# Early-fusion block on one core: scores and values of two steps issued together, other PSUM banks, another order of loads

## The chip, the cores and the metric

The kernel runs on one core of a Trainium2 chip. The time is the device time in microseconds (us) of one execution. TensorE (PE) multiplies and transposes into PSUM, which has eight banks of 512 fp32 per partition; VectorE (DVE) and ScalarE (ACT) read PSUM; GpSimd (POOL) works on SBUF; SyncE (SP) only issues transfers. Each engine works through its own list of instructions in order, and semaphores tie the lists together.

## The reference

```python
h = concat([cls, patches(x) @ W.T + b]) + pos_enc      # per image: 1 + 36 tokens
h = concat([h, txt])                                   # T = 114 tokens of D = 256
n = layernorm(h)
q, k, v = n @ Wq, n @ Wk, n @ Wv                       # 16 heads of 64
a = softmax(causal(q @ k.T / 8)) @ v
h = h + (n + a @ Wo)
n = layernorm(h)
gates = softmax(n @ router_w + router_b)               # 8 experts, top 2
# each expert takes up to 570 tokens, in their order
h = h + sum_e gate_e * (gelu(n_e @ w1[e] + b1[e]) @ w2[e] + b2[e])
```

There are 32 images (3 x 96 x 96) with 77 text tokens each. All is fp32; the products of the projections and of the experts are made of three fp32r products each (high x high, low x high, high x low), so each operand is kept as a high and a low part.

## The kernel before

**Groups and steps.** Attention goes over 8 groups of 4 images (`body(g)`, once for every engine). A group has 16 pairs of heads and images and is written as 19 steps `n`. At step `n` PE does four things, in this order: the scores of pair `n` (L1229, into `score_bank`), the values of pair `n - 3` (L1249, into `o_bank`, below also W), the transposes of the probabilities of pair `n - 2` (L1238, into `pT_bank`, below also T), and then a projection (lines L380 to L382, six matmuls of the helper `halves`, into one of three banks `bank`). Up to step 12 that projection is K or Q of a later head pair. The scores are below also S, the projection P.

**Work between the steps.** At step 3 the next group's patches are transposed (jobs E), at step 8 the last group's normalised rows (jobs Y, L1147), at step 12 come the router's logits (job L, L1262), at step 13 the next group's tokens (jobs X, L1147), ahead of that step's scores. Steps 14 to 16 hold the first halves of the next group's V, steps 17 and 18 the second halves (V1, V3 and then V5, V7 as PE counts them). After step 18 come the patch embedding (L1127, into `score_bank0`), the count of places (job C), the output projection (jobs O) and Q, K, Q of the next group.

**The other engines at a step.** ACT at step `n`: the drain of a K projection if `n` is odd, `oT_hi` of pair `n - 3` (L693), the copy `pT` of pair `n - 2` (L697), the four exponentials of pair `n` (L703). At step 9 it also drains a Y job, at step 10 it packs the pixels of group `g + 2` (`tok`, L642). DVE at step `n`: the drain of a Q projection if `n` is even, mask and maximum of pair `n` (L980), `nb` (L984), the reciprocal `rc` of pair `n - 1` (L988), `oT_lo` of pair `n - 3` (L781), then pieces of statistics, normalisation and routing. POOL normalises pair `n - 1` (L570).

**Banks.** `Jobs` lists all jobs that use `bank` in PE's order; job `i` takes bank `i % len(bank)`, and PE waits at its first matmul until job `i - len(bank)` has been drained:

```python
def bank_free(self, name, k):
    i = self.index(name, k) - len(bank)
    return self.emptied(i) if i >= 0 else []
```

**SP.** In the start SP loads the weights and the pixels of groups 0 and 1, then clears the slots in DRAM (8 transfers of 605.6 KB and one of 570 KB, L436 and L437), and then enters `body(0)`: pixels of group 2 (L398, L406), text of group 1 (L409). DVE needs that text at step 7 (statistics of `hraw`).

**Experts.** After the 8 groups the experts' stage runs with all 8 banks; the change only renames its banks.

## Time and profile before

| | |
|---|---|
| median of 3 runs | 967.36 us (965.38 to 967.66) |
| profiled execution | 964.54 us, span 962.6 us, mean granted clock 0.958 |
| PE busy | 869.2 us (90%) |
| DVE, ACT, POOL busy | 555.8, 516.0, 370.4 us |
| chain that ended last | PE 76%, SP's queue 5%, DVE 5%, POOL 4%, ACT 4% |

Busy time is counted by engine; idle time of an engine matters only where another waits for it. The chain that ended last is followed back from the last instruction, at each step to what released it. The step names above are not in the trace: they are found by the order of the rows, since each step has one group of L1229, L1249 and L1238 rows.

### The profile page before, as it was taken

The numbers are of one execution on the slowest core, as the hardware profiler recorded it, in microseconds if no ns is written. First come the engines' busy times: TensorE is split into PE (matmuls) and PEld (weight loads), VectorE is DVE, ScalarE is ACT, GpSimd is POOL, SyncE is SP. The second block draws the span as 40 slices with busy tenths as digits, with TensorE's granted clock in tenths as the row PEclk, the third lists the DMA queues.
The fourth block names the chain that finished last, engine by engine and source line by source line (L and its number), as shares of the span: only waits on it lengthen the run. The fifth ranks groups of instructions, "written<-read, shape, count | busy, mean of one in ns | idle before, by whom it ended". The sixth has DMA issues, their size and how long they took to land.

```text
span 962.6 us, 19817 instructions
## 1 busy us (share of the span) xinstructions
PE 869.2 (90%) x6897; PEld 753.9 (78%) x6897; DVE 555.8 (58%) x2433; ACT 516.0 (54%) x1686; POOL 370.4 (38%) x677
## 2 busy tenths in 40 slices
PE   4895899999999999999999999998617999999996
PEld 3674697788778779778877877876617999999996
DVE  3563428645753853764575375476326777777771
ACT  3373808825952880782495288087005555555551
POOL 2132305426425534542642554454430333222333
PEclk9797999999999999999999999999757999999998
DMA  8442101102011111110200110100125654444422
GB/s 253 118 131 78 39 1 35 38 13 64 11 29 44 33 38 39 37 39 8 59 1 1 33 35 2 37 1 2 24 90 165 165 124 127 96 131 109 94 26 25
DMA packets 61907, 57.64 MB, mean 60 GB/s; under 512 B 26783, under 2 KB 56651, under 8 KB 61696
## 3 DMA queue, kind: packets, MB, share of 16 engines
q1 hardware_dynamic: 41170, 45.15, 15.3%
q0 software_dynamic: 18944, 9.76, 6.3%
q10 hardware_dynamic: 1696, 1.49, 0.6%
q8 instruction: 55, 0.90, 0.4%
q14 instruction: 42, 0.34, 0.1%
HBM read 34.25 MB, written 21.89 MB: 58 GB/s over the span
## 4 chain that ended last, share of the span: by engine, by line
PE 76%; SPq 5%; DVE 5%; POOL 4%; ACT 4%; issue 3%; DMA 2%; ACTq 1%; POOLq 0%; DVEq 0%
PE bank L380 13%; PE bank L382 12%; PE bank L381 12%; PE pT_bank L1238 6%; PE o_bank L1249 6%; PE score_bank L1229 6%; PE score_bank L1127 3%; SPq L436 3%; POOL pr L570 2%; PE o_bank L380 2%; PE o_bank L381 2%; PE o_bank L382 2%; PE score_bank L380 2%; PE score_bank L381 2%; PE score_bank L382 2%
## 5 line engine op out<-in xcount | busy, mean ns | idle before, releaser
L570 POOL TENSOR_SCALAR pr<-pr,rc 114x114 f32<-114x114 f32 x512 | 179.3, 370 | 244.9 <-DVE rc L988 244.9
L703 ACT ACTIVATE pr<-sm,nb 114x114 f32<-114x114 f32 x512 | 192.2, 379 | 34.9 <-DVE nb L984 33.5
L980 DVE CUSTOM_DVE_ANT_0 sm<-score_bank,mask 114x114 f32<-114x114 f32 x512 | 110.5, 272 | 52.9 <-PE score_bank L1229 52.8
L601 POOL DMA_INDIRECT out_dram<-yout,dest x40 | 74.0, 1851 | 164.0 <-ACT yout L755 162.5
L551 POOL DMA_INDIRECT slots_dram<-rows,slot x64 | 72.8, 1138 | 128.0 <-DVE slot L947 93.3
L621 ACT ACTIVATE kT<-bank 128x456 f32<-128x456 f32 x64 | 34.1, 533 | 146.8 <-PE bank L382 146.8
L1229 PEld LDWEIGHTS score_bank<-kT,qT 64*114 64x114 f32 x1024 | 61.8, 176 | 56.7 <-issue 34.7
L380 PE MATMUL bank<-xT_hi,wqkv_hi 128*128 128x456 f32 x256 | 104.0, 406 | 0.0
L1229 PE MATMUL score_bank<-kT,qT 64*114 64x114 f32 x1024 | 84.5, 283 | 20.6 <-DVE mx L980 17.5
L703 ACT ACTIVATION_READ_ACCUMULATOR pr<-sm,nb 114x1 f32 x512 | 97.1, 190 | 0.0
L381 PE MATMUL bank<-xT_lo,wqkv_hi 128*128 128x456 f32 x256 | 94.5, 369 | 0.0
L382 PE MATMUL bank<-xT_hi,wqkv_lo 128*128 128x456 f32 x256 | 94.5, 369 | 0.0
L1238 PE MATMUL pT_bank<-ident,pr 114*114 114x114 f32 x512 | 78.3, 276 | 10.3 <-POOL pr L570 10.3
L697 ACT ACTIVATE pT<-pT_bank 114x456 f32<-114x456 f32 x128 | 70.6, 551 | 23.2 <-PE pT_bank L1238 23.0
L1249 PE MATMUL o_bank<-pT,vv 114*64 114x114 f32 x1024 | 79.5, 277 | 2.3 <-ACT pT L697 2.1
L1238 PEld LDWEIGHTS pT_bank<-ident,pr 114*114 114x114 f32 x512 | 49.6, 136 | 30.5 <-POOL pr L570 14.5
L380 PE MATMUL bank<-wo_hi,oT_hi 128*114 128x256 f32 x256 | 73.1, 286 | 0.0
L382 PE MATMUL bank<-wo_hi,oT_lo 128*114 128x256 f32 x256 | 72.6, 283 | 0.0
L381 PE MATMUL bank<-wo_lo,oT_hi 128*114 128x256 f32 x256 | 72.4, 283 | 0.0
L693 ACT ACTIVATE oT_hi<-o_bank 128x228 fp32r<-128x228 f32 x128 | 45.7, 357 | 47.0 <-PE o_bank L1249 47.0
L1249 PEld LDWEIGHTS o_bank<-pT,vv 114*64 114x64 f32 x1024 | 51.1, 138 | 23.0 <-issue 8.1
L781 DVE TENSOR_TENSOR oT_lo<-o_bank,oT_hi 128x228 fp32r<-128x228 f32 x128 | 47.9, 374 | 33.9 <-ACT oT_hi L693 33.4
(198 smaller groups left out, 2227.0 us busy)
## 6 DMA issues: line engine op xcount, KB each, us to landing
stage_a<-in_L_ffn_w_dram SPq DMA_DIRECT2D x8, 1024.0 KB, 5.1
stage_b<-in_L_ffn_w_dram SPq DMA_DIRECT2D x8, 1024.0 KB, 7.2
slots_dram<-fill SPq DMA_DIRECT2D x8, 605.6 KB
xs<-slots_dram SPq DMA_DIRECT2D x8, 605.6 KB
pix<-in_x_dram SPq DMA_DIRECT2D x96, 36.0 KB, 2.2
hraw<-in_txt_dram SPq DMA_DIRECT2D x8, 308.0 KB
out_dram<-h SPq DMA_DIRECT2D x8, 308.0 KB
pix<-pix SPq DMA_DIRECT2D x7, 216.0 KB, 2.5
```

The source lines that it names most:

```text
L380: pe.matmul(out_ap, a[0], b[0], start=start, stop=False)
L381: pe.matmul(out_ap, a[0], b[1], start=False, stop=False)
L382: return pe.matmul(out_ap, a[1], b[0], start=False, stop=stop)
L551: pool.indirect_dma_start(slots, bass.IndirectOffsetOnAxis(ap=slot[:, j, b:b + 1], axis=0), rows[k % 2][:, b, :], None, bounds_check=E * C ...
L570: p = pool.tensor_scalar(pr[:, m % 4, i, :], pr[:, m % 4, i, :], rc[:, m % 4, i:i + 1], 1.0, ALU.mult, ALU.mult)
L601: pool.indirect_dma_start(out, bass.IndirectOffsetOnAxis(ap=dest[e % 2][:, t:t + 1], axis=0), yout[:, t, :], None, compute_op=ALU.add).the ...
L697: act.activation(pT[:, m % 2, :, :], pT_bank[0:T, 0:4 * T].rearrange("p (i q) -> p i q", i=4), ACT.Copy).then_inc(pT_copied, 1)
L703: a = act.activation(pr[:, n % 4, i, :], sm[:, n % 2, i, :], ACT.Exp, bias=nb[:, n % 2, i:i + 1], scale=SCALE, accum_out=rs[:, n % 4, i:i ...
L980: m = dve.tensor_tensor_reduce(sm[:, n % 2, i, :], score_bank[i % 2][0:T, i // 2 * T:(i // 2 + 1) * T], mask[:, :], 1.0, NEG, ALU.add, ALU ...
L1229: m = pe.matmul(score_bank[h][0:T, b * T:(b + 1) * T], qT[head, c % 2, tokens], kT[head, c % 2, tokens], start=True, stop=True)
L1238: m = pe.transpose(pT_bank[0:T, i * T:(i + 1) * T], pr[:, n % 4, i, :], ident[0:T, 0:T])
L1249: m = pe.matmul(o_bank[n % 2][h * DK:(h + 1) * DK, b * T:(b + 1) * T], vv[:, b0 + b, v0:v0 + DK], pT[:, n % 2, 2 * b + h, :], start=True, ...
```

## The change

`bank` has two banks instead of three, and `pT_bank` two instead of one. PE issues scores at even steps only, for pairs `n` and `n + 1`, into 456 columns of each score bank instead of 228, and values at even steps only, for pairs `n - 4` and `n - 3`; ACT and DVE take `oT_hi` and `oT_lo` of the same two pairs at even steps. DVE's maximum of a pair waits for the scores of both. DVE drains all four second halves of V at step 18 instead of two at step 17 and two at step 18. SP loads each group's text ahead of the pixels, and clears the slots inside `body(0)`, behind both.

```diff
@@ -198,9 +198,9 @@
         def psum(name):
             return ctx.enter_context(nc.psum_tensor(name, [128, 512], F32))
-        bank = [psum(f"bank{i}") for i in range(3)]
+        bank = [psum(f"bank{i}") for i in range(2)]
         score_bank = [psum(f"score_bank{i}") for i in range(2)]
-        pT_bank = psum("pT_bank")
+        pT_bank = [psum(f"pT_bank{i}") for i in range(2)]
         o_bank = [psum(f"o_bank{i}") for i in range(2)]
@@ -247,7 +247,7 @@
         AT_E, AT_Y, AT_L, AT_X = 3, 8, 12, 13
         V_FIRST = {AT_X + 1: (0,), AT_X + 2: (1, 2), AT_X + 3: (3,)}
-        V_SECOND = {PAIRS + 1: (0, 1), PAIRS + 2: (2, 3)}
+        V_SECOND, V_DRAINED = {PAIRS + 1: (0, 1), PAIRS + 2: (2, 3)}, {PAIRS + 2: (0, 1, 2, 3)}
         STATS2, MOMENTS2, NORM2 = {1: (0, 1), 2: (2, 3)}, 3, {5: (0, 1), 6: (2, 3)}
         STATS1, MOMENTS1, NORM1 = {7: (0, 1), 8: (2, 3)}, 8, {10: (0, 1), 11: (2, 3)}
@@ -345,7 +345,7 @@
-        ebanks = bank + score_bank + [pT_bank] + o_bank
+        ebanks = bank + score_bank + pT_bank + o_bank
@@ -431,19 +431,22 @@
             sp.dma_start(router_bb[:, :, :], router_b.rearrange("(o b e) -> o b e", o=1, b=1).broadcast_to([T, GB, E])).then_inc(small_in, 16)
             sp.wait_ge(packed, 1)
             load_pixels(1)
-            sp.wait_ge(fill_done, 2)
-            for e in range(E):
-                sp.dma_start(slots[e * CAP:(e + 1) * CAP, :].rearrange("(t p) r -> p t r", p=T), fill[:, :, :]).then_inc(slots_cleared, 16)
-            sp.dma_start(out[B * T:B * T + CAP, :].rearrange("(t p) r -> p t r", p=T), fill[:, :, 0:D]).then_inc(slots_cleared, 16)
+            def clear_slots():
+                sp.wait_ge(fill_done, 2)
+                for e in range(E):
+                    sp.dma_start(slots[e * CAP:(e + 1) * CAP, :].rearrange("(t p) r -> p t r", p=T), fill[:, :, :]).then_inc(slots_cleared, 16)
+                sp.dma_start(out[B * T:B * T + CAP, :].rearrange("(t p) r -> p t r", p=T), fill[:, :, 0:D]).then_inc(slots_cleared, 16)
             def body(g, first=False, last=False):
                 jobs = Jobs(g)
+                if not last:
+                    sp.wait_ge(hx_done, 2 * g + 2)
+                    load_text(g + 1)
                 if g < G - 2:
                     sp.wait_ge(packed, g + 2)
                     load_pixels(g + 2)
-                if not last:
-                    sp.wait_ge(hx_done, 2 * g + 2)
-                    load_text(g + 1)
+                if first:
+                    clear_slots()
                 if not first:
                     wait_all(sp, jobs.emptied(jobs.last_before("O", 1)))
                     set_out(g - 1)
@@ -679,22 +682,22 @@
                                 drain_x(jobs, k)
                         for b in V_FIRST.get(n - 1, ()):
                             drain_v(jobs, b)
-                    if 3 <= n:
-                        m = n - 3
-                        c, b = m // 2, 2 * (m % 2)
-                        if first and m == 0:
-                            act.wait_ge(filled, len(START_JOBS))
-                            act.wait_ge(wk_lo, 1)
-                            act.wait_ge(wo_lo_done, 1)
-                            act.wait_ge(cls_in, 16)
-                        act.wait_ge(o_done, pair(g, m + 1))
-                        act.activation(oT_hi[:, c, b * T:(b + 2) * T], o_bank[m % 2][:, 0:2 * T], ACT.Copy).then_inc(o_hi, 1)
+                    if first and n == 4:
+                        act.wait_ge(filled, len(START_JOBS))
+                        act.wait_ge(wk_lo, 1)
+                        act.wait_ge(wo_lo_done, 1)
+                        act.wait_ge(cls_in, 16)
+                    if n % 2 == 0:
+                        for m in (n - 4, n - 3):
+                            if 0 <= m:
+                                c, b = m // 2, 2 * (m % 2)
+                                act.wait_ge(o_done, pair(g, m + 1))
+                                act.activation(oT_hi[:, c, b * T:(b + 2) * T], o_bank[m % 2][:, 0:2 * T], ACT.Copy).then_inc(o_hi, 1)
                     if 2 <= n < PAIRS + 2:
                         m = n - 2
                         act.wait_ge(pT_done, pair(g, m + 1))
-                        act.activation(pT[:, m % 2, :, :], pT_bank[0:T, 0:4 * T].rearrange("p (i q) -> p i q", i=4), ACT.Copy).then_inc(pT_copied, 1)
+                        act.activation(pT[:, m % 2, :, :], pT_bank[m % 2][0:T, 0:4 * T].rearrange("p (i q) -> p i q", i=4), ACT.Copy).then_inc(pT_copied, 1)
                     if n < PAIRS:
                         act.wait_ge(bias_done, pair(g, n + 1))
                         if not (first and n < 4):
@@ -975,9 +978,9 @@
                             drain_x(jobs, k)
                     if n < PAIRS:
-                        dve.wait_ge(scores_done, 2 * pair(g, n + 1))
+                        dve.wait_ge(scores_done, 2 * pair(g, n + 2 - n % 2))
                         for i in range(4):
-                            m = dve.tensor_tensor_reduce(sm[:, n % 2, i, :], score_bank[i % 2][0:T, i // 2 * T:(i // 2 + 1) * T], mask[:, :],
+                            m = dve.tensor_tensor_reduce(sm[:, n % 2, i, :], score_bank[i % 2][0:T, (2 * (n % 2) + i // 2) * T:(2 * (n % 2) + i // 2 + 1) * T], mask[:, :],
                                                          1.0, NEG, ALU.add, ALU.max, mx[:, n % 2, i:i + 1])
                         m.then_inc(max_done, 1)
                         dve.wait_ge(max_done, pair(g, n + 1))
@@ -986,12 +989,12 @@
                         dve.wait_ge(exp_done, pair(g, n))
                         dve.reciprocal(rc[:, (n - 1) % 4, :], rs[:, (n - 1) % 4, :]).then_inc(recip_done, 1)
-                    if 3 <= n:
-                        m = n - 3
-                        c, b = m // 2, 2 * (m % 2)
-                        dve.wait_ge(o_hi, pair(g, m + 1))
-                        split_low(oT_lo[:, c, b * T:(b + 2) * T], o_bank[m % 2][:, 0:2 * T], oT_hi[:, c, b * T:(b + 2) * T], o_lo)
+                    if n % 2 == 0:
+                        for m in (n - 4, n - 3):
+                            if 0 <= m:
+                                c, b = m // 2, 2 * (m % 2)
+                                dve.wait_ge(o_hi, pair(g, m + 1))
+                                split_low(oT_lo[:, c, b * T:(b + 2) * T], o_bank[m % 2][:, 0:2 * T], oT_hi[:, c, b * T:(b + 2) * T], o_lo)
                     if not first:
                         for b in STATS2.get(n, ()):
                             statistics(b, h2, st2, stats2)
@@ -1016,7 +1019,7 @@
                             dve.wait_ge(hx_done, 2 * g + 2)
                         for b in NORM1.get(n, ()):
                             normalise(b, xn[:, b, :], hraw[:, b, :], mv1, rstd1, xn_done)
-                        for b in V_SECOND.get(n, ()):
+                        for b in V_DRAINED.get(n, ()):
                             drain_v(jobs, b)
                 if not last and not (isinstance(g, int) and g == G - 2):
                     drain_embedded(g + 2)
@@ -1217,25 +1220,25 @@
                     wait_all(pe, jobs.emptied(jobs.last_before("K", 0) if c == 0 else jobs.index("K", c)))
                     wait_all(pe, jobs.emptied(jobs.last_before("Q", c) if c < 2 else jobs.index("Q", c)))
-                if n == 0 and g < G - 1:
-                    pe.wait_ge(embT_done, g + 2)
-                else:
-                    pe.wait_ge(max_done, pair(g, n))
+                    if n == 0 and g < G - 1:
+                        pe.wait_ge(embT_done, g + 2)
+                    else:
+                        pe.wait_ge(max_done, pair(g, n))
                 for b in range(2):
                     tokens = slice((b0 + b) * T, (b0 + b + 1) * T)
                     for h in range(2):
                         head = slice(h * DK, (h + 1) * DK)
-                        m = pe.matmul(score_bank[h][0:T, b * T:(b + 1) * T], qT[head, c % 2, tokens], kT[head, c % 2, tokens], start=True, stop=True)
+                        m = pe.matmul(score_bank[h][0:T, tokens], qT[head, c % 2, tokens], kT[head, c % 2, tokens], start=True, stop=True)
                         if b == 1:
                             m.then_inc(scores_done, 1)
             def transpose_probs(g, n, first):
                 pe.wait_ge(normed, pair(g, n + 1))
-                if not (first and n < 1):
-                    pe.wait_ge(pT_copied, pair(g, n))
+                if not (first and n < 2):
+                    pe.wait_ge(pT_copied, pair(g, n - 1))
                 for i in range(4):
-                    m = pe.transpose(pT_bank[0:T, i * T:(i + 1) * T], pr[:, n % 4, i, :], ident[0:T, 0:T])
+                    m = pe.transpose(pT_bank[n % 2][0:T, i * T:(i + 1) * T], pr[:, n % 4, i, :], ident[0:T, 0:T])
                 m.then_inc(pT_done, 1)
             def weigh_values(g, n, first):
@@ -1279,10 +1282,14 @@
                         pe.wait_ge(xn_done, GB * (g + 2))
                         for k in range(KC):
                             transpose_tokens(jobs, "X", xn, k)
-                    if n < PAIRS:
-                        scores(g, n, jobs, first)
-                    if 3 <= n:
-                        weigh_values(g, n - 3, first)
+                    if n % 2 == 0:
+                        for m in (n, n + 1):
+                            if m < PAIRS:
+                                scores(g, m, jobs, first)
+                        for m in (n - 4, n - 3):
+                            if 0 <= m:
+                                weigh_values(g, m, first)
                     if 2 <= n < PAIRS + 2:
                         transpose_probs(g, n - 2, first)
                     if n < LAST_QK:
```

What stands in a row of PE's list at step 18 of a steady group, before (pair 15's values, then V5 and the first matmul of V7; "waits" names the semaphores, `act_drained` and `dve_drained` count drained jobs):

```order
L1249 MATMUL o_bank1<-pT_80,vv_77 64x114 [waits o_lo,pT_copied]
L1249 MATMUL o_bank1<-pT_80,vv_77 64x114 x3
L380 MATMUL bank1<-wqkv_hi_60,xT_hi_73 114x512 [waits act_drained]
L381 MATMUL bank1<-wqkv_lo_61,xT_hi_73 114x512
L382 MATMUL bank1<-wqkv_hi_60,xT_lo_74 114x512
L380 MATMUL bank1<-wqkv_hi_60,xT_hi_73 114x512
L381 MATMUL bank1<-wqkv_lo_61,xT_hi_73 114x512
L382 MATMUL bank1<-wqkv_hi_60,xT_lo_74 114x512
L380 MATMUL bank2<-wqkv_hi_60,xT_hi_73 114x512 [waits dve_drained]
```

and now, with the values of pairs 14 and 15 ahead of V5 and V7:

```order
L1252 MATMUL o_bank0<-pT_80,vv_77 64x114 [waits o_lo,pT_copied]
L1252 MATMUL o_bank0<-pT_80,vv_77 64x114 x3
L1252 MATMUL o_bank1<-pT_80,vv_77 64x114 [waits o_lo,pT_copied]
L1252 MATMUL o_bank1<-pT_80,vv_77 64x114 x3
L380 MATMUL bank0<-wqkv_hi_60,xT_hi_73 114x512 [waits dve_drained]
L381 MATMUL bank0<-wqkv_lo_61,xT_hi_73 114x512
L382 MATMUL bank0<-wqkv_hi_60,xT_lo_74 114x512
L380 MATMUL bank0<-wqkv_hi_60,xT_hi_73 114x512
L381 MATMUL bank0<-wqkv_lo_61,xT_hi_73 114x512
L382 MATMUL bank0<-wqkv_hi_60,xT_lo_74 114x512
L380 MATMUL bank1<-wqkv_hi_60,xT_hi_73 114x512 [waits dve_drained]
```

V5 waited for a drain of ACT (V6, three jobs back); it now waits for a drain of DVE (V1, two jobs back).

DVE's list at the same place, before, from the drains of V1 and V3 at step 17 on (`vv` is V, the rows with `chosen` and `before` are the routing of step 18):

```order
L785 COPY vv_77<-bank2 114x512 [waits filled,routed]
L785 COPY vv_77<-bank0 114x512 [waits filled]
L781 TENSOR_TENSOR oT_lo_82<-o_bank1,oT_hi_81 128x228 [waits o_hi]
L928 TENSOR_TENSOR chosen_110<-oh_109 114x32
L931 TENSOR_TENSOR before_111<-before_111,chosen_110 114x8 [waits routed] x4
L785 COPY vv_77<-bank1 114x512 [waits filled]
L785 COPY vv_77<-bank2 114x512 [waits filled]
```

and now:

```order
L784 TENSOR_TENSOR oT_lo_82<-o_bank0,oT_hi_81 128x228 [waits o_hi,routed]
L784 TENSOR_TENSOR oT_lo_82<-o_bank1,oT_hi_81 128x228 [waits o_hi]
L931 TENSOR_TENSOR chosen_110<-oh_109 114x32
L934 TENSOR_TENSOR before_111<-before_111,chosen_110 114x8 [waits routed] x4
L788 COPY vv_77<-bank0 114x512 [waits filled]
L788 COPY vv_77<-bank1 114x512 [waits filled]
L788 COPY vv_77<-bank0 114x512 [waits filled]
L788 COPY vv_77<-bank1 114x512 [waits filled]
```

The drains of V1 and V3 have moved behind both `oT_lo` and behind the routing of step 18.

PE's list at steps 13 and 14 of a steady group, before, from the second X transposes to the scores of pair 14:

```order
L1147 MATMUL bank0<-ident_49,xn_70 128x114 [waits act_drained]
L1147 MATMUL bank0<-ident_49,xn_70 128x114 x3
L1229 MATMUL score_bank0<-kT_76,qT_75 114x114 [waits max_done]
L1229 MATMUL score_bank1<-kT_76,qT_75 114x114
L1229 MATMUL score_bank0<-kT_76,qT_75 114x114
L1229 MATMUL score_bank1<-kT_76,qT_75 114x114
L1249 MATMUL o_bank0<-pT_80,vv_77 64x114 [waits o_lo,pT_copied]
L1249 MATMUL o_bank0<-pT_80,vv_77 64x114 x3
L1238 MATMUL pT_bank<-ident_49,pr_79 114x114 [waits pT_copied,normed]
L1238 MATMUL pT_bank<-ident_49,pr_79 114x114 x3
L1229 MATMUL score_bank0<-kT_76,qT_75 114x114 [waits max_done,dve_drained,act_drained]
L1229 MATMUL score_bank1<-kT_76,qT_75 114x114
```

and now (the scores of pair 13 stand a step earlier, those of 14 and 15 together):

```order
L1150 MATMUL bank0<-ident_49,xn_70 128x114 [waits act_drained,xn_done]
L1150 MATMUL bank0<-ident_49,xn_70 128x114 x3
L1150 MATMUL bank1<-ident_49,xn_70 128x114 [waits dve_drained]
L1150 MATMUL bank1<-ident_49,xn_70 128x114 x3
L1241 MATMUL pT_bank1<-ident_49,pr_79 114x114 [waits pT_copied,normed]
L1241 MATMUL pT_bank1<-ident_49,pr_79 114x114 x3
L1232 MATMUL score_bank0<-kT_76,qT_75 114x114 [waits max_done,dve_drained,act_drained]
L1232 MATMUL score_bank1<-kT_76,qT_75 114x114
L1232 MATMUL score_bank0<-kT_76,qT_75 114x114
L1232 MATMUL score_bank1<-kT_76,qT_75 114x114
```

Between the X transposes and the scores of pair 14, which wait for DVE's maximum of pair 13, only one group of transposes is left where three groups of work stood.

## Rows read from the trace of the kernel before

**Rows 1.** The page's first line.

```profile
span 962.6 us, 19817 instructions
```

**Rows 2.** Timeline of SP's queue, 25 to 90 us: start, length, line, issues.

```profile
33.34 29.74 SPq L436 DMA_DIRECT2D slots_dram<-fill  x8
...
68.18 12.10 SPq L398 DMA_DIRECT2D pix<-in_x_dram  x12
...
82.34 0.53 SPq L409 DMA_DIRECT2D hraw<-in_txt_dram  x1
```

**Rows 3.** Timeline of DVE in group 0; in brackets the idle time before.

```profile
85.83 0.75 DVE L806 BATCH_NORM_STATS2 st<-hraw 114x6 f32<-114x256 f32 x2 [13.06 <-DMA hraw<-in_txt_dram]
```

**Rows 4.** Timeline of PE in group 0: scores of steps 8, 9 and 14.

```profile
87.95 1.11 PE L1229 MATMUL score_bank<-kT,qT 64*114 64x114 f32 x8 [11.45 <-DVE mx L980]
...
92.83 0.66 PE L1229 MATMUL score_bank<-kT,qT 64*114 64x114 f32 x8
...
106.86 0.66 PE L1229 MATMUL score_bank<-kT,qT 64*114 64x114 f32 x8 [2.10 <-DVE mx L980]
```

**Rows 5.** Timeline of PE, one steady group from its first scores to the next group's.

```profile
304.83 0.66 PE L1229 MATMUL score_bank<-kT,qT 64*114 64x114 f32 x8
...
324.58 0.66 PE L1229 MATMUL score_bank<-kT,qT 64*114 64x114 f32 x8
...
325.17 0.61 PE L1249 MATMUL o_bank<-pT,vv 114*64 114x114 f32 x8
...
325.71 0.60 PE L1238 MATMUL pT_bank<-ident,pr 114*114 114x114 f32 x4
...
327.49 0.66 PE L1229 MATMUL score_bank<-kT,qT 64*114 64x114 f32 x8
...
334.11 0.66 PE L1229 MATMUL score_bank<-kT,qT 64*114 64x114 f32 x8
...
340.51 0.66 PE L1229 MATMUL score_bank<-kT,qT 64*114 64x114 f32 x8 [0.52 <-ACT kT L621]
...
344.95 1.08 PE L1147 MATMUL bank<-ident,xn 114*128 114x114 f32 x8
...
348.33 0.66 PE L1229 MATMUL score_bank<-kT,qT 64*114 64x114 f32 x8 [0.63 <-DVE mx L980]
...
350.38 0.47 PE L380 MATMUL bank<-wqkv_hi,xT_hi 128*114 128x512 f32 x1
...
363.24 0.50 PE L380 MATMUL bank<-wqkv_hi,xT_hi 128*114 128x512 f32 x1
...
366.12 4.08 PE L1127 MATMUL score_bank<-tok,embW 96*128 96x144 f32 x32
...
385.38 0.66 PE L1229 MATMUL score_bank<-kT,qT 64*114 64x114 f32 x8
```

**Rows 6.** Instructions of line L1229, 320 to 330 us: min/median/max ns.

```profile
L1229 PE MATMUL score_bank<-kT,qT x24: 258/260/350, 321.7 to 327.9; 64*114 64x114 f32 x24
```

**Rows 7.** Timeline of ACT in the same group.

```profile
326.35 0.55 ACT L697 ACTIVATE pT<-pT_bank 114x456 f32<-114x456 f32 x1 [0.16 <-PE pT_bank L1238]
...
335.88 0.55 ACT L697 ACTIVATE pT<-pT_bank 114x456 f32<-114x456 f32 x1 [0.16 <-PE pT_bank L1238]
...
337.82 2.20 ACT L642 ACTIVATE tok<-pix 96x1152 f32<-96x1152 f32 x1
...
339.93 0.53 ACT L621 ACTIVATE kT<-bank 128x456 f32<-128x456 f32 x1
```

**Rows 8.** Timeline of POOL in the same group.

```profile
326.56 1.39 POOL L570 TENSOR_SCALAR pr<-pr,rc 114x114 f32<-114x114 f32 x4 [1.44 <-DVE rc L988]
```

**Rows 9.** Timeline of DVE in the same group, at step 18.

```profile
363.75 0.40 DVE L781 TENSOR_TENSOR oT_lo<-o_bank,oT_hi 128x228 fp32r<-128x228 f32 x1 [0.25 <-ACT oT_hi L693]
364.06 0.18 DVE L928 TENSOR_TENSOR chosen<-oh 114x32 bf16<-114x32 f32 x1
364.28 0.75 DVE L931 TENSOR_TENSOR before<-before,chosen 114x8 bf16<-114x8 bf16 x4
364.95 0.68 DVE L785 COPY vv<-bank 114x512 f32<-114x512 f32 x1
```

## The prediction

> **What bounds the kernel now.** I read the page first, then SP's queue, then PE's timeline in group 0 and in one steady group, then ACT, POOL and DVE beside it. The span is 962.6 us [rows 1]. In group 0 DVE sat idle 13.06 us until the text of group 1 had landed [rows 3]; its issue stands at 82.34 us, behind the slot clearing (29.74 us for eight issues from 33.34 on, then one more) and 12.10 us of pixel issues [rows 2]. PE waited 11.45 us for DVE's maximum, and its scores then took 1.11 us a block instead of 0.66: step 8 lasted from 87.95 to 92.83, 4.88 us [rows 4]. In a steady group PE is the bound: 80.55 us from 304.83 to 385.38, and a plain step (324.58 to 327.49) is 2.91 us: scores 0.59, values 0.54, transposes with a projection 1.78, with no wait [rows 5]. Only two kinds of waits show in its rows: 0.52 us for ACT's drain of K (after the packing) and 0.63 us for DVE's maximum (after the X jobs) [rows 5]. So what the change saves on PE counts, but what it makes PE wait for counts as well.
>
> **Text ahead of clearing.** The nine clearing transfers and the pixels no longer stand ahead of the text. The text goes out when `hx` of group 0 is made; SP has nothing else queued ahead of it, and DVE first looks for it at 72.8 us (85.83 less 13.06) [rows 3]. The wait of 11.45 us goes, and the half clock behind it: step 8 costs 2.91 instead of 4.88 us [rows 4, 5]. Gain 11.45 + 1.97 = 13.4 us. The clearing now lies beside groups 0 and 1; behind it on SP stand the text of group 2 and group 0's output, wanted a group later. Cost nothing; without that cover it would cost what the text costs now.
>
> **What merging saves on PE.** A block of scores has 8 matmul records; the row is 0.66 us long, one record lasts 0.26 [rows 5, 6], so their starts lie 0.40 / 7 = 0.057 us apart and 8 of them fill 0.46 us, while a block takes 0.59. Values in the same way: (0.61 - 0.26) / 7 x 8 = 0.40 of 0.54. A second block behind one of its kind should cost 0.46 and 0.40. Two steps then take 0.59 + 0.46 + 0.54 + 0.40 + 2 x 1.78 = 5.55 us instead of 5.82. Bounds: the gap may belong to every block (saves 0), or the gap between projection and scores may go too (some 0.1 more). I take 0.27.
> The Trainium skill (TensorEngine Tiling (Array Packing), Key Properties) says that changing the tiling mode drains TensorE. Scores use 64-row tiles, values 64-column ones, transposes the whole array; by that rule a merged pair has three changes fewer and takes about 5.45 us, and if the gap belonged to every block instead it would take 5.82. No row separates the two.
>
> **What takes it back in a plain pair of steps.** POOL's normalisation of pair n - 1 starts 1.98 us after the scores of step n (326.56 against 324.58) and lasts 1.39 [rows 5, 8], since DVE takes the reciprocal behind the maximum of pair n. That maximum now waits for both blocks, 0.46 later: 1.98 + 0.46 + 1.39 + 0.06 = 3.89 us, where PE wants those transposes at 1.05 + 0.94 + 1.78 = 3.77. A pair of steps takes 3.89 + 1.78 = 5.67, only 0.15 less than before.
> ACT loses slack. At an even step its two `oT_hi` and `pT` wait for values and transposes of PE, which start at 1.05 + 0.94 = 1.99. `pT` starts 0.64 later (325.71 to 326.35), the exponentials end 1.94 after its start (335.88 to 337.82) [rows 5, 7]: 4.57, and the drain of K behind them 0.53 + 0.05: 5.15, against 4.3 before. That is in time for 5.67, but not for the four places below. Times count from a block of scores; S0, S10 are the scores of pairs 0, 10.
>
> - **S0 to S10, before 29.28 us.** The first exponentials start 0.46 later and the transposes of pairs 0 and 1 with them; nothing lies ahead to hide it. At step 3 the second E job needs Q's bank, issued just before it. Together about +0.55, each partly hidden. At step 8 the second Y job takes the bank of the K just issued, drained only at 5.15 where PE wants it at 4.2; with 0.44 for the transposes and 1.78 that makes a pair of 7.37. Two plain pairs and this: 18.7 against 18.25, +0.5.
> - **S10 to S12, before 6.40.** ACT packs pixels for 2.11 us (337.82 to 339.93) ahead of K's drain [rows 7]: 5.15 + 2.11 = 7.26. +0.86, in groups 0 to 5.
> - **S12 to the first V, before 9.87.** One more block of scores and of values go ahead of X: 4.44 + 0.86 = 5.30. From X to the scores of pair 14 it stays 3.38 us (344.95 to 348.33), which ends with DVE's maximum of pair 13 behind both `xT_lo`; but PE has only one group of transposes left to do in it, and waits some 2.0 (3.38 less 1.0 of X and 0.37) instead of 0.63 [rows 5]. Then 1.99 + 0.37. Sum 11.04, +1.17.
> - **First V to the embedding, before 15.74 (350.38 to 366.12).** Gone from it: scores of pair 15 (0.59) and twice 0.14: 14.87. New: V5 needs V1's bank, which DVE drains behind both `oT_lo` and the routing. Before, V5 started at 363.24 and `oT_lo` of pair 15 at 363.75, 0.51 later; the routing ends 1.20 after that (364.95), the drain takes 0.68 [rows 5, 9]. PE waits 0.51 + 1.20 + 0.68 + 0.06 = 2.45. Sum 17.32, +1.58. V7, C, O and the next Q and K find their banks drained: 1.4 us or more of PE's work lies between each and its drain. The 19.26 us to the next group stay.
>
> Groups 1 to 5: 0.55 + 0.5 + 0.86 + 1.17 + 1.58 = 4.66 each, 23.3. Group 0 has no Y job, no logits and no routing: 0.55 - 0.4 + 0.86 + 0.7 + 0.7 = 2.4. Group 6 doesn't pack: 3.7. Group 7 has neither X nor V: about 1.1 (Y, and pairs 14 and 15 later behind the logits). Sum 30.5 us; the second `pT` bank saves nothing, since `pT` was copied in time. Stages outside attention are left as they are.
>
> **Sum.** 964.54 + 30.5 - 13.4 = 981.6 us, against the profiled execution's own time, which lies 2.8 us under the median of the runs; I forecast 983.
>
> **Rivals.**
> (a) As worked out: 983, its own range 972 to 994 (merging saves nothing: 64 pairs x 0.27 = 17, of which waits already swallow about half, +9; waits in part hidden: -11). Chance 0.52.
> (b) The same, and the waits also cost the clock. After 11.45 us of idling the granted clock was at its lower level and a step cost 1.97 more; after 2.10 us of idling scores still took 0.66 [rows 4]. The waits of 2.45 us (groups 1 to 6) lie between these. If each of the six is followed by such a stretch: +12, 995; if the seven of 2.0 as well: 1008. Chance 0.15. The Trainium skill (TensorE: Matmul & The Clock Gate, HAM oscillation) names idle gaps between bursts of matmuls as what puts the array back to half clock; by it these waits could do so.
> (c) Faster: merged blocks on PE are cheaper than their records' pace. Everything above hangs on the start of the even step's transposes, so a saving of x more in each pair of blocks comes back 64 times (8 a group). From x = 0.25 the change is even, from 0.30 measurably faster; with x = 0.4, 983 - 26 = 957. Against it: the second blocks would have to cost 0.46 together, and records 0.057 apart show no room. For it: the change of shape between blocks may cost more than rows show. Chance 0.18, with all other ways to less than 13 us of loss in it.
> (d) Losses and the gain cancel: if the wait for V1 and the one after X cost half, 30.5 becomes 17, 968. Chance 0.10.
> (e) The text move does nothing, since something else holds step 7 of group 0 (the `hx` release, or SP's issues): 983 + 13 = 996. Against it: rows 2 and 3 name transfer and place. Chance 0.05.
>
> **Numbers.** A measurement of this kernel tells about 0.3%, 2.9 us. Faster 0.18 (c), same 0.10 (d), slower 0.72 (a, b, e). The range leaves out the far half of (b) and the far third of (c): 956 to 1000.
>
> **What the changed kernel's profile would show.** Text: DVE's wait of 13 us at step 7 of group 0 is gone, the text issues ahead of the pixels and of the clearing. Merging: rows of scores x16 about 1.1 us long, values starting 1.05 after them; a plain pair of steps near 5.67 us with a small wait of PE for POOL at the odd step. Waits of PE: for ACT's K drain at step 8 (about 1.0) and at step 12 (1.6), for DVE's maximum at step 14 (2.0), for DVE's drain of V1 at step 18 (2.45, and 1.6 in group 0). A steady group of 85.2 us. Wrong if: the steady group is under 82.5 us, the granted clock leaves its full level in groups 1 to 6, or the wait at step 18 is under 1 us.

## The result, and the profile after

The changed kernel takes **1002.4 us** (median of 4 runs, 999.36 to 1003.81) against 967.25 for the kernel before on the same chip: ratio 1.0363, 95% interval 1.0336 to 1.0390. It is 35 us slower, where the forecast of 983 us meant 16, and lies above its range of 956 to 1000. The profiled execution is 997.4 us long, 34.8 more than before [rows 1].

The page of the changed kernel: span, busy times, granted clock in 40 slices, the chain that ended last, and two groups of PE rows with their idle time.

```profile
span 997.4 us, 19801 instructions
...
PE 867.5 (87%) x6897; PEld 764.9 (77%) x6897; DVE 553.2 (55%) x2433; ACT 515.2 (52%) x1686; POOL 371.8 (37%) x677
...
PEclk9899999999899989989998999999755999999999
...
PE 74%; DVE 8%; ACT 6%; issue 5%; POOL 4%; DMA 1%; SPq 1%; POOLq 0%; DVEq 0%; ACTq 0%
...
L1232 PE MATMUL score_bank<-kT,qT 64*114 64x114 f32 x1024 | 71.5, 281 | 26.9 <-DVE mx L983 14.9
...
L380 PE MATMUL bank<-wqkv_hi,xT_hi 128*114 128x512 f32 x128 | 59.6, 465 | 17.2 <-DVE vv L788 15.7
```

PE waits 14.9 us for DVE's maximum ahead of scores and 15.7 us for DVE's drains of V. SP's queue, 5% of the chain before, is down to 1%. The PEclk line is the first sign of something that the sum did not hold: one slice with an 8 in each of groups 2 to 5, where the kernel before has none.

SP's queue, 50 to 110 us, to be read against [rows 2]:

```profile
58.05 0.32 SPq L409 DMA_DIRECT2D hraw<-in_txt_dram  x1
58.41 7.69 SPq L398 DMA_DIRECT2D pix<-in_x_dram  x12
...
68.25 30.20 SPq L437 DMA_DIRECT2D slots_dram<-fill  x8
98.48 4.87 SPq L438 DMA_DIRECT2D out_dram<-fill  x1
```

The text goes out at 58.05 instead of 82.34, and DVE's wait of 13.06 us is gone; that part of the change does what it says. Now the time by groups, each from its first scores to the next group's. A row gives start and end, length, then busy time and count of PE, its weight loads, DVE, ACT and POOL, then the granted clock, the DMA share and GB/s. Before (groups 0, 1 and 6, then group 7 with all that follows; groups 2 to 5 read like 1):

```profile
50.80:143.75 92.95, 77.66 (x611) 63.29 (x610) 38.87 (x209) 46.41 (x175) 25.85 (x67) 0.93 0.21 61
143.75:224.29 80.54, 78.16 (x635) 64.27 (x634) 47.32 (x252) 47.34 (x177) 36.16 (x76) 1.00 0.13 34
...
546.47:622.43 75.96, 74.00 (x604) 60.26 (x603) 47.01 (x251) 45.47 (x176) 36.12 (x76) 1.00 0.08 21
622.43:962.60 340.17, 293.02 (x2355) 280.92 (x2354) 211.56 (x681) 170.21 (x436) 117.82 (x123) 0.91 0.34 84
```

The changed kernel (groups 2, 4 and 5 read like 3):

```profile
51.05:133.79 82.74, 74.64 (x611) 62.43 (x610) 38.67 (x209) 46.58 (x175) 25.93 (x67) 0.98 0.28 83
133.79:218.31 84.52, 75.50 (x636) 63.73 (x635) 46.81 (x252) 46.93 (x177) 36.43 (x76) 1.00 0.12 32
...
307.07:395.80 88.73, 79.69 (x635) 67.16 (x635) 47.11 (x252) 47.33 (x177) 36.30 (x76) 0.94 0.12 31
...
573.29:656.39 83.10, 74.40 (x603) 62.19 (x602) 46.54 (x251) 45.05 (x176) 36.31 (x76) 0.96 0.08 20
656.39:997.40 341.01, 289.96 (x2355) 279.97 (x2354) 210.88 (x681) 170.17 (x436) 117.82 (x123) 0.92 0.34 84
```

Group 0 is 10.2 us shorter, group 1 is 4.0 longer at full clock, groups 2 to 5 are 8.2 longer each with a granted clock of 0.94, group 6 is 7.1 longer; start and tail give 1.1. Sum: -10.2 + 4.0 + 32.8 + 7.1 + 1.1 = 34.8.

**Group 1 against group 3.** Group 1 shows the waits alone. Its four stretches that the forecast names (S0 to S10, S10 to S12, to the first V, to the embedding), in the same columns:

```profile
133.79:163.92 30.13, 27.02 (x238) 21.70 (x237) 22.99 (x135) 22.56 (x92) 13.58 (x34) 1.00 0.22 57
163.92:171.11 7.19, 5.63 (x53) 4.46 (x52) 5.57 (x30) 6.91 (x22) 5.40 (x13) 1.00 0.00 0
171.11:181.95 10.84, 8.86 (x107) 8.00 (x107) 5.63 (x38) 8.47 (x34) 2.77 (x8) 1.00 0.01 2
181.95:199.04 17.09, 14.72 (x95) 10.94 (x94) 8.63 (x41) 8.43 (x30) 4.16 (x12) 1.00 0.00 1
```

PE in it:

```profile
161.71 0.51 PE L1150 MATMUL bank<-ident,rows 114*128 114x114 f32 x3 [0.91 <-ACT kT L624]
...
171.11 1.06 PE L1232 MATMUL score_bank<-kT,qT 64*114 64x114 f32 x16 [1.18 <-ACT kT L624]
...
179.66 1.06 PE L1232 MATMUL score_bank<-kT,qT 64*114 64x114 f32 x16 [1.98 <-DVE mx L983]
...
196.17 0.49 PE L380 MATMUL bank<-wqkv_hi,xT_hi 128*114 128x512 f32 x1 [2.37 <-DVE vv L788]
196.50 0.40 PE L381 MATMUL bank<-wqkv_lo,xT_hi 128*114 128x512 f32 x1
...
199.04 0.65 PE L1130 MATMUL score_bank<-tok,embW 96*128 96x144 f32 x4
```

These are the four waits that the forecast names: second Y job, step 12, pair 14, V5. Beside them stand one of 0.58 us for ACT at step 2 and one of 0.98 for POOL at step 3, inside the first stretch. The same places in group 3, where the waits are as long but the work behind them is not:

```profile
352.94 1.89 PE L1232 MATMUL score_bank<-kT,qT 64*114 64x114 f32 x16 [1.97 <-DVE mx L983]
354.76 1.79 PE L1252 MATMUL o_bank<-pT,vv 114*64 114x114 f32 x16
...
372.10 0.49 PE L380 MATMUL bank<-wqkv_hi,xT_hi 128*114 128x512 f32 x1 [2.37 <-DVE vv L788]
...
373.58 0.63 PE L381 MATMUL bank<-wqkv_lo,xT_hi 128*114 128x512 f32 x1
...
376.55 0.66 PE L1130 MATMUL score_bank<-tok,embW 96*128 96x144 f32 x4
```

The same 16 score matmuls last 1.89 us instead of 1.06, a V matmul 0.63 instead of 0.40. The clock granted there:

```profile
352.00:359.00 7.00, 6.06 (x41) 5.18 (x42) 3.90 (x32) 3.80 (x17) 2.77 (x8) 0.51 0.00 0
359.00:370.00 11.00, 10.73 (x77) 7.99 (x75) 4.02 (x21) 7.08 (x24) 2.77 (x8) 1.00 0.01 1
372.00:376.00 4.00, 3.90 (x10) 2.90 (x11) 1.33 (x3) 0.00 (x0) 0.00 (x0) 0.57 0.00 0
```

Half clock (1.2 GHz) for 6.8 us at the scores of pair 14 and for 3.4 us at V5, full clock (2.4 GHz) between. In slices of 1 us the first fall comes at 352.1, after 1.1 us of the wait and 0.8 ahead of the scores; the second comes at 372.6, 0.5 behind V5's start. From the scores of pair 14 to V5 group 1 needs 196.17 - 179.66 = 16.51 us, group 3 19.16: the first stretch costs 2.65. From V5 to the embedding 2.87 against 4.45: the second costs 1.58. Together 4.23, which is all of the difference of the two groups, 88.73 - 84.52. Both falls show in groups 2 to 5; group 0 has one of 3.4 us, group 6 two of 3.4, group 1 none.

### The profile page after: what moved, and what is told of

Read it like the earlier page. It is cut to its first block, busy times and chain, and to the rows that moved or that the text cites. A ratio compares the mean times of both kernels' runs of the same rounds, so it can differ in the third digit from the quotient of the medians.

```text
span 997.4 us, 19801 instructions
## 1 busy us (share of the span) xinstructions
PE 867.5 (87%) x6897; PEld 764.9 (77%) x6897; DVE 553.2 (55%) x2433; ACT 515.2 (52%) x1686; POOL 371.8 (37%) x677
## 3 DMA queue, kind: packets, MB, share of 16 engines
q1 hardware_dynamic: 41170, 45.15, 14.9%
## 4 chain that ended last, share of the span: by engine, by line
PE 74%; DVE 8%; ACT 6%; issue 5%; POOL 4%; DMA 1%; SPq 1%; POOLq 0%; DVEq 0%; ACTq 0%
PE bank L380 11%; PE bank L382 11%; PE bank L381 11%; PE score_bank L1232 7%; PE o_bank L1252 5%; PE pT_bank L1241 5%; ACT pr L706 4%; PE score_bank L1130 3%; POOL pr L573 3%; DVE sm L983 3%; PE pT_bank L380 2%; PE pT_bank L381 2%; PE pT_bank L382 2%; PE o_bank L381 2%; PE o_bank L382 2%
## 5 line engine op out<-in xcount | busy, mean ns | idle before, releaser
L1232 PE MATMUL score_bank<-kT,qT 64*114 64x114 f32 x1024 | 71.5, 281 | 26.9 <-DVE mx L983 14.9
L1241 PE MATMUL pT_bank<-ident,pr 114*114 114x114 f32 x512 | 79.1, 279 | 16.2 <-POOL pr L573 14.9
L1241 PEld LDWEIGHTS pT_bank<-ident,pr 114*114 114x114 f32 x512 | 53.0, 139 | 42.3 <-POOL pr L573 31.4
L380 PE MATMUL bank<-wqkv_hi,xT_hi 128*114 128x512 f32 x128 | 59.6, 465 | 17.2 <-DVE vv L788 15.7
L1252 PE MATMUL o_bank<-pT,vv 114*64 114x114 f32 x1024 | 69.5, 282 | 0.3 <-ACT pT L700 0.3
L784 DVE TENSOR_TENSOR oT_lo<-o_bank,oT_hi 128x228 fp32r<-128x228 f32 x128 | 44.5, 381 | 35.5 <-ACT oT_hi L696 35.5
```

The costliest lines, as they stand in the source:

```text
L380: pe.matmul(out_ap, a[0], b[0], start=start, stop=False)
L1232: m = pe.matmul(score_bank[h][0:T, tokens], qT[head, c % 2, tokens], kT[head, c % 2, tokens], start=True, stop=True)
L1241: m = pe.transpose(pT_bank[n % 2][0:T, i * T:(i + 1) * T], pr[:, n % 4, i, :], ident[0:T, 0:T])
L1252: m = pe.matmul(o_bank[n % 2][h * DK:(h + 1) * DK, b * T:(b + 1) * T], vv[:, b0 + b, v0:v0 + DK], pT[:, n % 2, 2 * b + h, :], start=True, ...
```

## The experiments

**The theories.** Clock theory: the four waits cost their length, as the forecast had it, and two of them, being idle, also bring PE's clock down. First rival: the half clock has another cause (the merged blocks, the load over time), and filling the waits changes nothing. Second rival: waits cost only their length, and the rest lies elsewhere. All times are medians of 4 runs or more, taken on several chips; the kernel before took 966.6 to 968.1 beside them, and the ratios are to that.

**SP's order alone.** The kernel before with the text and the clearing moved as in the change's diff, nothing else.

```diff
             load_pixels(1)
-            sp.wait_ge(fill_done, 2)
...
             def body(g, first=False, last=False):
                 jobs = Jobs(g)
+                if not last:
+                    sp.wait_ge(hx_done, 2 * g + 2)
+                    load_text(g + 1)
                 if g < G - 2:
                     sp.wait_ge(packed, g + 2)
                     load_pixels(g + 2)
...
+                if first:
+                    clear_slots()
```

> The kernel before with nothing but SP's new order: text ahead of pixels and of the clearing. By the forecast DVE's wait of 13.06 us for the text, PE's of 11.45 us behind it and the half clock after it (1.97 us) go: 967.3 - 13.4 = 954 us. Rival: something else holds step 7 of group 0, and the time stays at 967. The changed kernel's group 0 was only 10.2 us shorter than before, but that holds merged steps as well.

Measured 954.8 us, ratio 0.9866 [0.9847, 0.9885], against 967.7: -12.9 where -13.4 was forecast. The group of 92.95 us became 81.63, 11.3 less, since a half clock that was not there before now follows the wait ahead of pair 14 in it:

```profile
96.10 1.12 PE L1232 MATMUL score_bank<-kT,qT 64*114 64x114 f32 x8 [2.11 <-DVE mx L983]
```

(In the profiled executions the start, up to the first scores, is 2.8 us longer and the whole 9.0 shorter; it is the medians that differ by 12.9.) So all else in the change costs 1002.4 - 954.8 = 47.6 us, not the 30.5 of the sum.

**Waits filled with work.** The changed kernel, with matmuls in the two longest waits.

```diff
+            def fillers(dst, count):
+                for _ in range(count):
+                    pe.matmul(dst[:, :], wqkv_hi[:, 0, 0:128], wqkv_hi[:, 0, 0:512], start=True, stop=True)
...
+                if n == 14 and g < G - 1 and 7:
+
+                    pe.wait_ge(o_lo, pair(g, 10))
+                    fillers(o_bank[0], 7)
...
+                            if b == 2:
+                                pe.wait_ge(max_done, pair(g, PAIRS))
+                                fillers(score_bank[1], 8)
                             project_v(jobs, 2 * b + 1)
```

> The changed kernel with idle time on PE filled: 7 matmuls of 512 columns whose result nobody reads stand ahead of the scores of pair 14, and 8 ahead of V5. They wait for nothing new and take about 0.22 us each, so they lie inside the waits of 1.97 and 2.37 us. Clock theory: those waits, being idle, bring the granted clock to half for 6.7 and 3.4 us behind them in groups 2 to 5, which costs 88.75 - 84.52 = 4.23 us a group, some 3.5 in group 6 and 1.5 in group 0; with matmuls in them the clock stays full and the time is 1002.4 - 22 = 980 us. Rival: the half clock comes from something else (the merged blocks, the whole load over time); then it stays and so does the time, 1002 us or a little more.

Measured 980.2 us, ratio to before 1.0128 [1.0107, 1.0149]: 22.2 us less than the changed kernel although PE does 105 matmuls more. PE in its group 3, then its groups 1 and 3:

```profile
346.10 1.85 PE L1219 MATMUL o_bank<-wqkv_hi 128*128 128x512 f32 x7
348.31 1.06 PE L1240 MATMUL score_bank<-kT,qT 64*114 64x114 f32 x16 [0.36 <-DVE mx L983]
...
362.38 2.14 PE L1219 MATMUL score_bank<-wqkv_hi 128*128 128x512 f32 x8
364.83 0.49 PE L380 MATMUL bank<-wqkv_hi,xT_hi 128*114 128x512 f32 x1 [0.31 <-DVE vv L788]
```

```profile
133.30:217.86 84.56, 79.16 (x650) 66.36 (x649) 46.87 (x252) 46.96 (x177) 36.56 (x76) 1.00 0.12 32
302.42:386.94 84.52, 79.16 (x650) 66.34 (x649) 46.86 (x252) 46.95 (x177) 36.45 (x76) 1.00 0.12 33
```

Groups 1 to 5 now take 84.5 us each, and the granted clock is 1.00 in groups 0 to 6. The scores of pair 14 and V5 start as long after the group's first scores as they did in group 1 of the changed kernel (45.9 and 62.4 us); only the idling is gone. That rules out the first rival: the merged blocks are all there. The second goes as well. The kernel without the half clock is the one that the forecast costed, and it takes 980 where 983 was said. (The profiled executions differ by 18.9 us and not 22.2: that of the changed kernel is the fastest of its four.)

**Only V5's wait filled.** The same without the 7 matmuls.

> The changed kernel with the 8 filling matmuls ahead of V5 alone; the wait of 1.97 us ahead of the scores of pair 14 stays idle. Clock theory, one fall for each wait: the half clock of 3.4 us behind V5 goes (1.6 us each in groups 2 to 6), that of 6.8 us behind pair 14 stays: 1002.4 - 8 = 994. If the two waits bring the clock down only together, both falls go: 980.

Measured 994.6 us, ratio 1.0283 [1.0265, 1.0301]. The clock around V5 is full in every group (in group 3, 370 to 376 us: 1.00); at the scores of pair 14 it still falls, for 3.4 or 6.8 us, now in group 1 as well. So a fall needs only one of the two waits: filling V5's took 7.8 us off, filling that of pair 14 as well another 14.4.

**V1 and V3 drained first at step 18.** DVE drains them behind the values of pair 15, ahead of both `oT_lo` and the routing.

```diff
-        V_SECOND, V_DRAINED = {PAIRS + 1: (0, 1), PAIRS + 2: (2, 3)}, {PAIRS + 2: (0, 1, 2, 3)}
+        V_SECOND, V_DRAINED = {PAIRS + 1: (0, 1), PAIRS + 2: (2, 3)}, {PAIRS + 2: (2, 3)}
...
+                    if not last and n == PAIRS + 2:
+                        dve.wait_ge(o_done, pair(g, PAIRS))
+                        drain_v(jobs, 0)
+                        drain_v(jobs, 1)
                     if n % 2 == 0:
                         for m in (n - 4, n - 3):
```

> The changed kernel, but at step 18 DVE drains V1 and V3 right behind the values of pairs 14 and 15, ahead of both oT_lo and of the routing. The wait ahead of V5 falls from 2.37 to some 0.9 us, 1.4 less in groups 1 to 6 and 0.7 less in group 0: -9 us, 993, if waits cost only their length. If the half clock behind this wait (1.6 us each in groups 2 to 6) goes with it: -17 us, 985.

Measured 984.8 us (977.69 to 986.34), ratio 1.0155 [1.0112, 1.0199]. V5 in a steady group, then the clock at the scores of pair 14 and at V5:

```profile
367.22 0.48 PE L380 MATMUL bank<-wqkv_hi,xT_hi 128*114 128x512 f32 x1 [0.85 <-DVE vv L788]
```

```profile
348.00:355.00 7.00, 5.16 (x38) 4.53 (x39) 4.57 (x32) 3.42 (x14) 2.79 (x8) 0.53 0.00 0
366.00:371.00 5.00, 4.15 (x28) 3.27 (x25) 3.93 (x11) 0.72 (x2) 0.00 (x0) 1.00 0.00 0
```

V5's wait is 0.85 us, and no half clock follows in any group; pair 14 still has it in groups 0 to 6. V1 cannot be drained at step 17, as it was before: its half of V is what the values of pair 14 still read, and merging has put these into step 18. So the wait for V1 comes from merging as well as from the banks.

**Maximum of pair 13 first.** At step 13 DVE does maximum, `nb` and reciprocal ahead of the logits and of both `xT_lo`.

```diff
-                    if not first and n == AT_L + 1:
-                        route(jobs, g - 1, 0)
-                    if not last and n == AT_X:
-                        for k in range(KC):
-                            drain_x(jobs, k)
                     if n < PAIRS:
...
                     if 1 <= n <= PAIRS:
...
                         dve.reciprocal(rc[:, (n - 1) % 4, :], rs[:, (n - 1) % 4, :]).then_inc(recip_done, 1)
+                    if not first and n == AT_L + 1:
+                        route(jobs, g - 1, 0)
+                    if not last and n == AT_X:
+                        for k in range(KC):
+                            drain_x(jobs, k)
```

> The changed kernel, but at step 13 DVE takes the maximum of pair 13 and the reciprocal of pair 12 ahead of the logits and of both xT_lo. The wait ahead of the scores of pair 14 falls from 1.97 to some 0.3 us; X's drains come about 1 us later, which V0 doesn't see. -1.6 us in seven groups: 991, if waits cost only their length. If the half clock behind this wait (2.65 us each in groups 2 to 6, some 1.5 in group 0) goes too: -26 us, 977.

Measured 969.5 us, ratio 1.0024 [1.0010, 1.0038], 7 less than expected. The scores of pair 14 wait for nothing, and V5, in a steady group, as long as ever. The clock at V5 follows, in that group (3) and in group 4:

```profile
343.84 1.06 PE L1232 MATMUL score_bank<-kT,qT 64*114 64x114 f32 x16
...
360.50 0.50 PE L380 MATMUL bank<-wqkv_hi,xT_hi 128*114 128x512 f32 x1 [2.38 <-DVE vv L788]
```

```profile
360.00:364.00 4.00, 3.50 (x18) 2.85 (x19) 2.16 (x4) 0.00 (x0) 0.00 (x0) 1.00 0.00 0
444.00:448.00 4.00, 4.00 (x14) 3.00 (x13) 0.94 (x2) 0.00 (x0) 0.00 (x0) 0.57 0.02 4
```

Here the clock mostly holds behind the same wait of 2.38 us: it fell in groups 1 and 4 only, against groups 2 to 6 in the changed kernel, and groups 2, 3 and 5 took 82.63 to 82.65 us. The three falls fewer are worth 3 x 1.58 = 4.7 of the 7 us. The length of a wait alone does not decide.

**Both orders of DVE.**

> The changed kernel with both reorderings of DVE together (maximum of pair 13 ahead of the logits and of xT_lo; V1 and V3 drained ahead of oT_lo and routing). In the run with the first alone a group took 82.65 us where the clock held, with the wait of 2.38 ahead of V5; in the run with the second alone that wait was 0.85. So 82.65 - 1.53 = 81.1 us a group, and no half clock: 969.5 - 7 x 1.5 - 3 = 956 us. If the clock falls for another reason than these two waits, 960 to 965.

Measured 957.4 us, ratio 0.9888 [0.9870, 0.9906], 81.3 to 81.9 us a steady group, granted clock 1.00 in groups 0 to 6. As expected, and already 1.1% faster than before, with banks and merging as in the change.

**The banks alone.** SP's new order, and the banks two and two, steps not merged.

```diff
-        bank = [psum(f"bank{i}") for i in range(3)]
+        bank = [psum(f"bank{i}") for i in range(2)]
-        pT_bank = psum("pT_bank")
+        pT_bank = [psum(f"pT_bank{i}") for i in range(2)]
```

> The kernel before with SP's new order (954.8 us) and the banks of the changed kernel (two and two), steps not merged, V drained as before. If the banks alone bring the waits ahead of the second E and the second Y (0.29 and 0.91 us in the changed kernel): 954.8 + 7 x 1.2 = 963. If those waits come from ACT's later drains under merging, nothing: 955. The wait ahead of V5 can't come back here, since V1 is drained a step earlier.

Measured 976.4 us, ratio 1.0086 [1.0069, 1.0102]: 21.5 above SP's order alone, where 8 were expected at most. Waits of PE in its group 2, and the clock behind the last of them (one of 0.74 us for POOL, which the kernel before has too, and one of 0.55 near the group's end are not shown):

```profile
227.62 0.61 PE L1142 MATMUL bank<-ident,embT 128*36 128x128 f32 x4 [0.29 <-DVE qT L788]
...
244.08 0.61 PE L1150 MATMUL bank<-ident,rows 114*128 114x114 f32 x4 [0.92 <-ACT kT L624]
...
253.94 0.66 PE L1232 MATMUL score_bank<-kT,qT 64*114 64x114 f32 x8 [0.52 <-ACT kT L624]
...
258.94 0.97 PE L1150 MATMUL bank<-ident,xn 114*128 114x114 f32 x8 [0.41 <-ACT kT L624]
```

```profile
260.00:267.00 7.00, 7.00 (x45) 5.37 (x46) 4.00 (x24) 4.94 (x21) 2.77 (x8) 0.54 0.01 2
```

The waits for E and Y are those of the changed kernel, and with three banks they are gone (below), so they belong to the banks. I had not expected one ahead of X, nor that group 1 would take 83.01 us at full clock (2.47 more, of which the waits make 1.7), nor half clock behind the X jobs of groups 2 and 3 (group 0 has it with SP's order alone as well). Groups 2 to 5 took 336.8 us together, 4 x 2.47 + 4.7 above before: 4.4 of the last term is the half clock of two of them. Another 3.3 us lie behind group 6 (343.0 us against 339.7 with SP's order alone), where the granted clock from 670 to 702 us was 0.68 against 0.84 at the same place (651 to 683).

**Merging alone.** The changed kernel with three projection banks and one for transposed probabilities.

> The changed kernel with the banks of before (three for projections, one for transposed probabilities) and nothing else: merged steps, text ahead, DVE's order as it is. Against the run with both reorderings of DVE (939.4) the wait of 1.97 us ahead of the scores of pair 14 comes back in seven groups (+12) and, by the clock theory, the half clock of 6.8 us behind it (2.65 us in six groups, +16); V5 has no wait, since its bank is V6's, drained by ACT. 967 us. If the clock holds with this one wait, 952. The fourth corner of a square with the kernel with SP's order alone (954.8), that with the two-and-two banks (976.4) and the changed kernel (1002.4).

Measured 973.1 us, ratio 1.0066 [1.0043, 1.0090]; 967 was expected. The clock falls at the scores of pair 14 in groups 1 to 6, and the last V job waits 0.80 us for DVE, which I had left out. In its group 0 the wait ahead of pair 14 is 2.71 us, more than in any other of these kernels, and the granted clock stayed at 1.00. The four kernels with SP's new order can now be set side by side: neither banks nor merging 954.8, banks alone +21.5, merging alone +18.3, both +47.6, that is 7.8 more than the two added.

**Merging with three banks and both orders of DVE.**

> The same, and the banks of before: three for projections, one for transposed probabilities; steps merged by two as in the changed kernel. Tells what the banks cost from what the merging costs. The waits that hang on a projection bank go (0.29 ahead of the second E, 0.91 ahead of the second Y, 0.85 ahead of V5): 81.1 - 2.05 = 79.05 us a group against 80.55 before, 956 - 14 = 942 us. Rival: with one pT bank the transposes of the odd step wait for ACT's copy of the even one (0.5 us in each of 8 pairs of steps): 956 - 14 + 28 = 970.

Measured **939.4 us**, ratio 0.9709 [0.9693, 0.9725], 78.93 us a steady group. The rival of 970 us is ruled out: with one `pT_bank` PE waits nowhere for ACT's copy in a steady group, so a second one saves nothing, as the forecast had it. One wait stands out, at step 12:

```profile
323.06 1.06 PE L1236 MATMUL score_bank<-kT,qT 64*114 64x114 f32 x16 [1.44 <-ACT kT L624]
```

**The packing at step 16 as well.** Besides three banks, merging and both orders of DVE:

```diff
-        AT_PACK = 10
+        AT_PACK = 16
```

> The fastest so far (three banks, merged, both reorderings of DVE, 939.4 us) with ACT's packing of pixels (2.11 us) at the end of step 16 instead of step 10. The wait for K's drain ahead of the scores of pair 12, 1.44 us in six groups, goes, since the drain then comes where the forecast put it without packing, 5.15 us after the even step's scores: -8 us, 931. If the packing then delays V6's drain or pT of pair 15 behind it, as much comes back in steps 17 and 18: 939.

Measured **929.5 us**, ratio 0.9611 [0.9595, 0.9627], the fastest kernel of the study, 3.9% faster than the kernel before. The wait at step 12 is gone and nothing took its place; a steady group:

```profile
282.15:359.62 77.47, 75.18 (x636) 63.77 (x635) 47.01 (x252) 46.64 (x177) 36.40 (x76) 1.00 0.13 36
```

**What merging is worth when nothing takes it back.** First SP's order with the maximum of pair 13 first, not merged, three banks.

> The kernel before with SP's new order and with the maximum of pair 13 ahead of the logits and of xT_lo on DVE; no merging, banks as before. The wait ahead of the scores of pair 14, 0.63 us in groups 1 to 6, shrinks to nothing: -3.8. In group 0 of the run with SP's order alone it was 2.11 us, and 6.82 us at half clock followed: -1.6 - 2.5. Sum 947 us. If POOL's normalisation of pair 12 takes the place of that wait, 952 to 955.

Measured 946.1 us, ratio 0.9777 [0.9761, 0.9794]. Then with the packing at step 16, which leaves merging (with the drain of V that it forces) as the only difference to the 929.5 us.

> The kernel before with SP's new order, the maximum of pair 13 first on DVE, and the packing at step 16; steps not merged, three banks and one. It is the 929.5 us kernel without the merging. The 0.52 us wait for K's drain at step 12 goes: 946.05 - 3.1 = 943. By the forecast merging saves 0.27 us in a pair of steps where nothing takes it back, 8 pairs of steps in 8 groups: 17 us; by the measured plain pairs (5.66 against 5.82) 10 us. So the merged kernel should be 10 to 17 us faster than this one. If its gain came from the banks or orders alone, this one takes 930 as well.

Measured 941.8 us, ratio 0.9729 [0.9713, 0.9745]; a steady group:

```profile
287.38:366.51 79.13, 77.92 (x635) 64.27 (x634) 46.82 (x252) 47.08 (x177) 36.05 (x76) 1.00 0.13 35
```

Merging is worth 12.3 us (11.4 by the two ratios, since the two kernels ran on different chips), 1.66 a steady group, or 0.21 for each of its 8 pairs of steps. PE's busy time falls by 2.7 us a group, so about 1 us of it still goes into waits.

## Why the forecast was wrong

The direction was right, and so were the costs of the base case at full clock. What is missing is the half clock: filling the two waits took it away with 22.2 us, and it had been rival (b), at 0.15 against 0.52. Step by step:

| | forecast | measured |
|---|---|---|
| text ahead of clearing | -13.4 | -12.9, alone (group 0: -11.3) |
| plain pair of steps | 5.67 us | 5.66 (324.25 to 329.91 in group 3) |
| S0 to S10 | +1.05 | +0.85 (group 1: 30.13) |
| S10 to S12 | +0.86 | +0.79 (7.19) |
| S12 to first V | +1.17 | +0.97 (10.84) |
| first V to embedding | +1.58 | +1.35 (17.09) |
| steady group at full clock | 85.2 us | 84.5 |
| half clock in a steady group | 0 | +4.2 (groups 2 to 5) |

- **Right: the waits and their places.** V5 2.45 forecast and 2.37 measured, pair 14 2.0 and 1.97, the second Y job 1.0 and 0.91, step 12 1.6 and 1.18. With the idling filled, the kernel is 12.5 us slower than before, against the forecast's 983 - 967 = 16.
- **The step that failed** is the one in rival (b): "after 2.10 us of idling scores still took 0.66 [rows 4]. The waits of 2.45 us (groups 1 to 6) lie between these." The sum, 964.54 + 30.5 - 13.4, has no term for the clock. I took one wait after which the clock had held as evidence that a wait of 2 us keeps it, and priced case (a) with full clock throughout. Measured in its place: half clock at both waits in groups 2 to 5, 4.2 us a group, and 22.2 us in all. The forecast's own marker, "the granted clock leaves its full level in groups 1 to 6", is what came. The kernel with SP's order alone shows how weak that evidence was: its wait of 2.11 us at the same place of group 0 was followed by half clock (granted clock 0.56 from 96 to 103 us).
- **The price in (b)** was 1.97 for each fall, taken from the half clock of group 0 before. Measured: 2.65 behind pair 14 and 1.58 behind V5, so 4.2 for both where (b) had 3.9. It gave 1008 with both kinds in all groups; groups 0 and 6 had shorter stretches and group 1 none, and 1002 came. The range stopped at 1000 by leaving out "the far half of (b)", and that half came.
- **Merging, 0.27 for a pair of steps:** 0.21 net between the kernels of 929.5 and 941.8 us. In a plain pair of the changed kernel the even step's transposes start 1.92 us behind the scores (324.25 to 326.17) where 1.99 was forecast, so rival (c), 0.4 more in each pair, is ruled out. The 0.07 did not shorten the pair: the odd step's transposes stand 3.89 behind the scores (328.14), exactly where the forecast put them by POOL.
- **The banks** were costed through the waits for E, Y and V1, and each of these was near in the changed kernel. Alone, though, they cost 21.5 us, of which 4.4 is half clock in groups 2 and 3 and 3.3 lies behind group 6.
- **A reading that was wrong:** "only two kinds of waits" in a steady group. The trace of the kernel before has two more, both for POOL, 0.74 us at 310.30 and 0.48 at 350.01. In the changed kernel the first has become 0.21 and 0.98, inside the +0.85 of the first stretch, and the second is gone.
- The Trainium skill (TensorE: Matmul & The Clock Gate, HAM oscillation), which the forecast set beside rival (b), names idle gaps between bursts of matmuls as what puts the array back to half clock. The filled waits agree, with 22.2 us. The waits for data in that page's example are longer than 1.97 and 2.37 us; that the clock also falls at waits as short as these is shown by the runs here.

Open: why the clock fell at these waits in groups 2 to 5 and not in group 1, whose rows ahead of them look the same; and why it mostly held behind V5's wait once that of pair 14 was gone. It is also open what part the work ahead of a wait has: the wait of pair 14 comes right behind the logits (16 matmuls of 8 columns) and transposes. Filling the waits shows that these falls needed the idling, and not that it was enough by itself. No run here tells.

## What to carry to other kernels

A new wait on PE costs its length, and can cost what the clock takes behind it as well, here 2.65 us for a wait of 1.97 and 1.58 for one of 2.37. One place in a trace where the clock held after such a wait is not evidence that it will; look at the granted clock in every stretch, and when a change adds waits of 2 us to a PE that had none over 0.74 us in a steady group, carry the half clock as a main case. Fewer banks and coarser steps both shift who must have drained by when: merging was worth 12 us here, but only after two of DVE's orders and one ACT job had been moved out of the way and the third bank was back.
